# A selective scan with three buffers for weighed states, five joined pairs, sums that trail by three, and ScalarE's work placed elsewhere in the tile

## The reference

```python
skip = xn @ skip_w.T                      # gate, from the normed input
x = silu(conv(xn @ in_w.T))               # 8 tiles of 128 channels
delta = softplus(x @ wd1.T @ wd2.T + wd2_b)
Bm, Cm = x @ wB.T, x @ wC.T               # 16 rows each
A = -exp(A_log)
h = exp(delta[:, :, None] * A) * h + (delta * x)[:, :, None] * B[:, None, :]   # a step of the scan
y = einsum('ben,bn->be', h, C)            # sum over the 16 states
y = (y + W_D * x) * silu(skip)
out = resid + y @ out_w.T
```

## Time and profile before

| | us |
|---|---|
| median of 3 runs | 2681.76 (2679.98 to 2691.23) |
| the profiled execution | 2680.32 |
| its span, first to last instruction | 2678.4 |
| scan stage, first key to last sum (87.8 to 485.8) | 398.0 |
| PE busy in 88 to 486 us | 385.76 |
| DVE busy in the same stretch | 368.39 |
| POOL busy | 325.62 |
| ACT busy | 260.49 |

### The profile page before, as it was taken

One profiled execution on the slowest core, in us unless ns is written; L12 is line 12 of the kernel. 1 busy time (PEld: TensorE's weight loads), 2 busy tenths in 40 slices (PEclk: granted clock), 3 DMA queues, 4 the chain that ended last, 5 costly groups with the idle time before them and its releaser, 6 DMA issues. The chain is left out here.

```text
span 2678.4 us, 31417 instructions
## 1 busy us (share of the span) xinstructions
PE 2415.5 (90%) x11965; PEld 1246.9 (47%) x11965; DVE 1352.9 (51%) x1929; ACT 921.5 (34%) x1896; POOL 635.7 (24%) x530
## 2 busy tenths in 40 slices
PE   7899999889999999888599799886998679999996
PEld 4444444344555555436345454353665333333332
DVE  5799999323788876731445412395444521111114
ACT  3666666014433334401122110186333212222221
POOL 0578888100000000001201100000000024444342
PEclk9999999889999999999799799998998789999998
DMA  3732222455444545326600100202000262560634
GB/s 106 242 102 88 85 95 76 104 200 177 153 154 161 167 117 168 110 85 228 218 1 0 43 0 3 77 20 94 1 1 4 71 240 96 204 277 27 244 113 146
DMA packets 97067, 301.31 MB, mean 112 GB/s; under 512 B 27114, under 2 KB 57990, under 8 KB 82204
## 3 DMA queue, kind: packets, MB, share of 16 engines
q1 hardware_dynamic: 63264, 171.06, 19.2%
q0 software_dynamic: 33664, 128.35, 13.3%
HBM read 446.13 MB, written 47.22 MB: 184 GB/s over the span
## 5 line engine op out<-in xcount | busy, mean ns | idle before, releaser
L772 POOL TENSOR_TENSOR x_rows<-ms_state,mb_C_everywhere 128x800 f32<-128x800 f32 x128 | 239.8, 1884 | 137.9 <-DVE ms_state L740 90.0
L1040 PE MATMUL psum<-at_Wv,at_context 128*128 128x512 f32 (+1 forms) x576 | 266.1, 601 | 0.0
L799 PE MATMUL psum<-mb_context,mb_key_w 128*128 128x361 f32 x768 | 252.6, 478 | 6.6 <-PEq L856 6.2
L740 DVE TENSOR_TENSOR_SCAN ms_state<-ms_decay,psum 128x800 f32<-128x800 f32 x128 | 233.0, 1820 | 19.4 <-ACT ms_decay L689 13.9
L3110 ACT ACTIVATE tf_hidden<-psum,tf_b 128x64 f32<-128x64 f32 x512 | 108.2, 362 | 356.5 <-PE psum L3067 356.5
L3056 PE MATMUL psum<-tf_W,tf_x_T 128*64 128x512 f32 x1024 | 229.1, 600 | 0.8 <-DVE tf_x_T L3119 0.8
L3078 PE MATMUL psum<-tf_W,tf_hidden 128*64 128x512 f32 x1024 | 226.4, 594 | 0.5 <-DMA tf_W<-in_L_W,tt_weight_row 0.5
L799 PEld LDWEIGHTS psum<-mb_context,mb_key_w 128*128 128x128 f32 x768 | 141.4, 191 | 120.9 <-issue 32.2
L1141 ACT ACTIVATE at_prob<-psum,at_neg_max 100x722 f32<-100x722 f32 x128 | 110.4, 863 | 145.7 <-DVE at_neg_max L1203 145.5
L2991 POOL DMA_INDIRECT tf_W<-in_L_W,tt_weight_row x120 | 119.4, 995 | 163.6 <-PE psum L3056 120.9
L1203 DVE TENSOR_REDUCE at_neg_max<-psum 100x1 f32<-100x722 f32 x128 | 115.5, 903 | 78.4 <-PE psum L1061 78.0
(11 more groups left out here) (485 smaller groups left out, 3689.5 us busy)
## 6 DMA issues: line engine op xcount, KB each, us to landing
at_piece<-in_L_W_f POOLq DMA_DIRECT2D x24, 1024.0 KB, 6.3
keys_dram<-x_rows SPq DMA_DIRECT2D x128, 180.5 KB, 1.9
at_k_cols<-keys_dram SPq DMA_DIRECT2D x64, 361.0 KB, 3.1
sf_W<-in_L_W SPq DMA_DIRECT2D x16, 1024.0 KB, 6.9
tf_W<-in_L_W SPq DMA_DIRECT2D x8, 2048.0 KB, 19.9
mb_context<-in_ctxT SPq DMA_DIRECT2D x16, 541.5 KB, 5.0
at_context<-in_ctxT SPq DMA_DIRECT2D x8, 1083.0 KB, 5.0
ternary_dram<-at_piece_made POOLq DMA_DIRECT2D x14, 512.0 KB, 4.0
```

Source lines behind the costliest of these rows:

```text
L740: nc.vector.tensor_tensor_scan(state[:, n % RH, :], decay[:, g % RA, :, :].rearrange("p b l -> p (b l)"), drive, 0.0, ALU.mult, ALU.add).t ...
L772: nc.gpsimd.tensor_tensor(slot(t, n), state[:, n % RH, :], cC[:, n, :], ALU.mult).then_inc(weighed, 1)
L799: last = nc.tensor.matmul(side("key", u, t == KE - 1)[:, 0:SH], lhsT=wk[:, k, e * P:(e + 1) * P], rhs=keys[:, h, k, :], start=(k == 0), st ...
L1040: last = nc.tensor.matmul(bank[0:rows_of(t), :], lhsT=ctxT[:, b % 2, k, t * P:t * P + rows_of(t)], rhs=wv[:, k, h * BANK:(h + 1) * BANK], ...
```

## The change

`RV` is 3 in place of 2, with a third buffer of `seen` of its own. `JOIN` has five steps, 1, 3, 5, 9 and 13, in place of four, 3, 5, 7 and 9. `TRAIL` is 3 in place of 2, so the block that makes keys 2m and 2m + 1 adds the states 2m - 3 and 2m - 2. Delta halves are made in blocks 1 and 2 in place of 0 and 1, gate halves in blocks 4 and 6 in place of 2 and 3. The tile before's sums are copied in step 5 in place of 4, x is scaled in step 8 and added in block 6 (before 6 and 5), GpSimd's product with the gate stands in step 6 in place of 2, and the Silu of the gate is the last thing of step 15 in place of the first of step 11.

```diff
-    RA, RH, RV, RS = 4, 4, 2, 2
+    RA, RH, RV, RS = 4, 4, 3, 2
...
-        gate, seen = part(0, 1), [part(1, 1), part(2, 1)]
+        gate, seen = part(0, 1), [part(1, 1), part(2, 1), sb("seen", [P, T])[:, :]]
...
-        COPY_AT, FINISH, SCALE, SUM_X, OPEN = 4, 2, 6, 5, 11
-        GATE_AT, DELTA_AT, LAG = [2, 3], [0, 1], 2
+        COPY_AT, FINISH, SCALE, SUM_X, OPEN = 5, 6, 8, 6, 15
+        GATE_AT, DELTA_AT, LAG = [4, 6], [1, 2], 2
...
-        JOIN = [3, 5, 7, 9]
-        TRAIL = 2
+        JOIN = [1, 3, 5, 9, 13]
+        TRAIL = 3
...
-                    if n == OPEN:
-                        take_key(t, n - LAG, last)
-                        act.wait_ge(side_taken, at_side(t, last, "gate", 1) + 1 + RS)
-                        nc.scalar.activation(gate, gate, ACT.Silu).then_inc(gated, 1)
                     act.wait_ge(scanned, i * per + g + 1 + (not first and g < per % RA))
...
-                    if n >= LAG and n != OPEN:
+                    if n >= LAG:
                         take_key(t, n - LAG, last)
-                    elif n < LAG and not first:
+                    elif not first:
                         take_key(t - 1, n - LAG + N_ST)
...
+                    if n == OPEN:
+                        act.wait_ge(side_taken, at_side(t, last, "gate", 1) + 1 + RS)
+                        nc.scalar.activation(gate, gate, ACT.Silu).then_inc(gated, 1)
```

## The result

The changed kernel took 2693.97 us (median of 11 runs, 2687.12 to 2700.77), the kernel before 2688.78 (11 runs, 2679.98 to 2691.85, the three shown before among them). The ratio, taken over the runs and not from the two medians (they lie 5.2 us apart), is 1.0024, 95% interval 1.0012 to 1.0035: 6.5 us slower, a loss that eleven runs of each tell from zero, under the half per cent that was counted as no change. The two profiled executions, 2680.32 and 2692.89 us, differ by 12.6; their scan stages, from the first key to the end of the last sum, by 7.5 (398.0 and 405.5). Nearly all of the rest lies behind the scan, where no instruction changed, and within the spread of the runs.

What follows compares the result with a forecast made beforehand. TensorE was taken to bound the scan, at 47.85 of 49.05 us a tile. Terms of +0.1 without the clock and +8.5 for its falls made +8.6 on 2680.32, 2688.9 us; range 2673 to 2699, the forecast's own 2683 to 2695.

Steps and rivals of the forecast that it cites:

- Which engine sets the pace: Scan tile of 49.05 us: TensorE's own work, 47.85 us, exceeds VectorE's 47.14, so TensorE sets the pace.
- The hole: TensorE before key 4, tiles 1 to 7: stands 2.26 us waiting for copied sums, +15.8 us, less 0.50 of before.
- The waits for joins: TensorE's three waits a tile for GpSimd's joins go: -8.3 us in seven tiles, -0.5 in the first.
- One join more for GpSimd: GpSimd pays 1.89 us more a tile, nothing on the path; TensorE adds one state fewer, -6.4 us over 8 tiles.
- The sum without the clock: Scan stage: the state saved, join waits gone and the wait for copies add up to +0.1 us.
- The clock: TensorE behind its holes: five of seven make the clock fall for the shorter time, +8.5 us.
- VectorE's wait moves to step 0: VectorE's 1.91 us wait for a decay moves from step 11 to step 0, costing nothing beyond TensorE's pace.
- The case without a hole: Rival: copies early or hidden, VectorE sets the pace at 47.14 us a tile; -12, about 2668 us; chance 0.08.

Runs made afterwards that it cites:

- e1: Changed kernel with TensorE's wait for the copied sums moved from state 0 to the first state it adds: 0.997 of the kernel before, stage 391.7 us.
- e4: Kernel before with only the Silu of the gate moved to the end of step 15: ratio 0.9997 to the kernel before, stage 399.1 us.
- e2: Changed kernel with two extra matmuls, results unread, in each TensorE hole before the wait for copies: 1.0008 of the kernel before, stage 397.6 us.
- e10: Changed kernel with GpSimd's weighing of state 14 put behind the next tile's dx: 1.0034 of the kernel before, stage 405.5 us.
- e7: e1 with GpSimd's weighing of state 14 put behind the next tile's dx: 0.9953 of the kernel before, stage 385.2 us.
- e3: Kernel before with only JOIN changed to five joins (1, 3, 5, 9, 13): ratio 1.0066 to the kernel before, stage 414.5 us.

## Why the prediction was right

The time, 2693.97 us, lay in the forecast's own range, 2683 to 2695, and the ratio on its side of 1. That the absolute time fell inside is luck in part: the forecast counted from 2680.32, and over eleven runs the kernel before took 2688.78, so the same +8.6 from there would have made 2697.4. The difference is the fairer test: +8.6 us forecast, +6.5 by the ratio, +7.5 in the stage. The steps can be checked one by one.

- *Which engine sets the pace.* TensorE, by 47.85 of 49.05 us. Right: each fall of the clock moved the tile by its full 1.70 us, TensorE's hole moved the stage (e1), and taking the Silu and a table load away from where VectorE waits (e4) gave nothing.
- *The hole.* Predicted 2.26 us from start to start and 2.1 in the records, in tiles 1 to 7; measured 2.24 (3.76 - 1.52) and 2.09, 14.6 us in 7, the last of them 2.00.
- *The waits for joins.* Predicted to go; they went, save one of 0.6 us.
- *One join more for GpSimd.* Costed at nothing, and wrong as a step, though the total did not show it. With less idle time GpSimd runs into dx, which took 1.3 to 1.8 us longer in tiles 1 to 3, so these tiles of VectorE took 48.4 to 49.5 us and not 47.2. It lay beside the hole in the changed kernel, which is why the sum held; with the hole gone (e1) it was the next limit. "GpSimd pays 1.89 us more, nothing on the path" should have asked what its idle time had been good for. In the kernel before, GpSimd was through with its work and stood waiting for dx while dx ran, seven times, 7.5 us, so the two hardly met: dx took 0.97 to 1.21 us. In tile 2 dx ran from 187.75 us, and then:

```profile
188.85 1.88 POOL L772 TENSOR_TENSOR x_rows<-ms_state,mb_C_everywhere 128x800 f32<-128x800 f32 x1 [1.09 <-DVE psum L731]
```

- *The sum without the clock.* Predicted +0.1, and e2 is the measurement: -0.4 in the stage.
- *The clock.* Predicted five falls of 1.7 us, 8.5; five came, 1.70 us each by the distances of key 4, and e2, which takes them away and leaves the hole's length, is worth 7.9 in the stage. The number five was taken from two idle times that went two ways, not worked out. That it came, here and in e10, is luck to a degree: 2.09 us were enough in one tile and not in the next, e10 had its five in other tiles, and other executions may have had more or fewer. The rule of the Trainium skill that the prediction names there is stated for longer waits than this hole, so it does not give seven falls here.
- *VectorE's wait moves to step 0.* Right from tile 4 on; before that it had decays in hand. In tiles 4, 5 and 6 a second wait of 0.9 us showed at step 11. The Silu alone does not move it (e4).
- *The case without a hole* was priced at -12 in all, with VectorE at 47.14 us a tile; its own terms, 11.4 and 2, make -13.4. e1 gave 6.3 in the stage, e7, which also frees dx, 12.8. The price was right for a kernel that needed one more edit.

## What to carry to other kernels

When an order written by hand is shifted by a step, go through every wait that is keyed to an index: a wait at the head of a function that may return at once binds whatever comes next in the engine's list, and a hole of 2 us in TensorE's list can cost another 1.7 by its clock. Before an engine off the critical path is given more work, ask which instruction of another engine runs undisturbed only because it idles. A change that seems to give nothing may be a gain and a loss of one size: here moving one line turned +0.24% into -0.3%, and a second line into -0.5%.

## What the runs showed of the hardware

- After a hole of 2.00 to 2.09 us in dense work the granted clock fell to 0.50 (1.2 GHz) for 3.4 us in five of seven tiles and held in two, and again in five of seven, not the same ones, in e10. Three waits of 1.63 us in e3 went both ways, one fall and two holds; e2's 0.55 us never made it fall. Each fall in the changed kernel cost 1.70 us (50.82 - 49.12).
- A VectorE tensor_tensor with both inputs in SBUF took 0.97 us alone and up to 2.75 beside a GpSimd tensor_tensor (e1, tiles 1 to 7: 1.78 to 2.69), and GpSimd's weighing grew from 1.88 to 2.68 where dx had begun before it, as at 235.94 us in the changed kernel:

```profile
234.61 2.23 DVE L730 TENSOR_TENSOR psum<-mb_delta,mb_conv_cols 128x800 f32<-128x800 f32 x1
```
```profile
234.10 1.88 POOL L771 TENSOR_TENSOR ms_seen<-ms_state,mb_C_everywhere 128x800 f32<-128x800 f32 x1 [2.26 <-PE psum L825]
235.94 2.68 POOL L771 TENSOR_TENSOR x_rows<-ms_state,mb_C_everywhere 128x800 f32<-128x800 f32 x1
```
